# Adding an attention mask by accumulating DMAs instead of by a TensorE product per head

## The reference

```
x = relu(x + dt * stencil(x))                                   # layer 0
y = up(expert(gelu(down(x)))) + x                               # layer 1, the adapter
x = (y - mean(y)) * rsqrt(var(y) + eps) * ln_gamma + ln_beta    # per row: the adapter norm
x = x + two matmuls, each before a silu of a whole-sequence norm  # layer 2
x = ln(x) * (1 + scale) + shift; q, k, v of 16 heads of 16      # layer 3
scores = q k^T / 4 + attention_bias                             # bias: 16 x 16 x 256 x 256, fp32
scores = where(mask, -inf, scores)                              # mask: one 256 x 256 per sequence
x = x + softmax(scores) v Wo;  x + ff(ln(x))
```

## Time and profile before

| | |
|---|---|
| median of three runs | 944.76 us (942.92 to 946.6) |
| the profiled execution | 941.49 us, of it span 939.7 us |
| mean granted clock of TensorE | 0.975 of full speed (1.00 from 150 us on) |
| DMA | 130.88 MB in 133081 packets, mean 139 GB/s |
| first head starts | about 92 us |

### The profile page before, as it was taken

The page is one execution under the profiler, slowest core; times in us unless marked ns, Lnnn a source line. Parts: engine busy times, 40 slices in busy tenths (PEclk is TensorE's granted clock), DMA queues, the critical chain, the costliest instruction groups (busy, mean ns, idle before and its releaser), DMA issues.

```text
span 939.7 us, 18088 instructions
## 1 busy us (share of the span) xinstructions
PE 858.8 (91%) x5646; PEld 661.4 (70%) x5731; DVE 751.3 (80%) x2375; ACT 731.6 (78%) x1901; POOL 239.2 (25%) x237
## 2 busy tenths in 40 slices
PE   7675869999999999999999999999999999998987
PEld 6353646777777777777777777777777777776766
DVE  7466788988898889888898888888898889876542
ACT  3123879979798888979798888979798888987773
POOL 1233213222223224222223224222223224120100
PEclk9678899999999999999999999999999999999999
DMA  9814545645446353644446363644447353645500
GB/s 252 246 54 114 173 125 146 177 138 152 114 122 193 102 162 103 191 133 139 127 124 191 103 160 103 193 139 139 121 127 189 106 159 103 179 136 150 154 13 22
DMA packets 133081, 130.88 MB, mean 139 GB/s; under 512 B 18265, under 2 KB 123481, under 8 KB 132969
## 3 DMA queue, kind: packets, MB, share of 16 engines
q1 hardware_dynamic: 101072, 111.49, 42.1%
q10 hardware_dynamic: 31914, 18.23, 6.8%
HBM read 112.61 MB, written 17.07 MB: 138 GB/s over the span
## 4 chain that ended last, share of the span: by engine, by line
PE 48%; ACT 23%; DVE 18%; issue 8%; POOL 1%; DMA 1%; ACTq 0%; DVEq 0%; POOLq 0%
PE ff_ps L1335 11%; PE PT_ps L1371 6%; ACT Pr L1057 5%; PE ff_ps L1316 5%; DVE bias L921 4%; PE ctx_ps L1393 4%; PE G L1216 4%; PE scores_ps L1356 4%; PE G L1139 3%; ACT L1057 3%; ACT tanh L1039 3%; ACT PT L1070 3%; ACT ffT L1043 3%; PE scores_ps L1353 2%; PE G L1212 2%
## 5 line engine op out<-in xcount | busy, mean ns | idle before, releaser
L1057 ACT ACTIVATE Pr<-bias,nmax 128x256 f32<-128x256 f32 x512 | 255.9, 506 | 41.9 <-DVE nmax L921 41.4
L921 DVE CUSTOM_DVE_ANT_0 bias<-scores_ps,bias 128x256 f32<-128x256 f32 x512 | 195.4, 420 | 60.0 <-issue 35.4
L1070 ACT ACTIVATE PT<-PT_ps 128x512 f32<-128x512 f32 x256 | 151.7, 593 | 50.3 <-PE PT_ps L1371 41.0
L1371 PE MATMUL PT_ps<-ident,Pr 128*128 128x128 f32 x1024 | 156.4, 275 | 9.0 <-ACT Pr L1057 9.0
L559 POOL TENSOR_TENSOR rstd<-var,half_neg 128x2 f32<-128x2 f32 (+1 forms) x64 | 42.7, 667 | 403.5 <-DVE var L684 256.4
L1371 PEld LDWEIGHTS PT_ps<-ident,Pr 128*128 128x128 f32 x1024 | 119.8, 141 | 18.4 <-ACT Pr L1057 15.0
L1316 PE MATMUL ff_ps<-ctxT,w 128*128 128x256 f32 x480 | 116.9, 386 | 10.7 <-ACT ffT L1043 8.9
L1335 PE MATMUL ff_ps<-w,ffT 128*128 128x256 f32 x480 | 114.8, 382 | 0.3 <-DVE ffT L898 0.3
L1316 PEld LDWEIGHTS ff_ps<-ctxT,w 128*128 128x128 f32 x480 | 86.3, 190 | 30.2 <-ACT ffT L1043 14.2
L1356 PE MATMUL scores_ps<-k_stack,q_stack 96*128 96x256 bf16 x512 | 99.2, 275 | 6.7 <-issue 3.3
L1057 ACT ACTIVATION_READ_ACCUMULATOR Pr<-bias,nmax 128x1 f32 x512 | 100.8, 197 | 0.0
(11 more groups left out here) (219 smaller groups left out, 1628.6 us busy)
## 6 DMA issues: line engine op xcount, KB each, us to landing
bias<-in_fside_Bx16xSxS_dram SPq DMA_DIRECT2D x256, 256.0 KB, 3.2
part_dram<-front ACTq DMA_DIRECT2D x32, 384.0 KB, 3.5
q_stack<-part_dram SPq DMA_DIRECT2D x32, 192.0 KB, 3.3
k_stack<-part_dram SPq DMA_DIRECT2D x32, 192.0 KB, 3.9
F<-in_x_dram SPq DMA_DIRECT2D x16, 256.0 KB, 3.7
ada<-rows_dram SPq DMA_DIRECT2D x16, 256.0 KB, 4.5
q_stack<-part_dram SPq DMA_DIRECT2D x32, 128.0 KB, 3.6
k_stack<-part_dram SPq DMA_DIRECT2D x32, 128.0 KB, 3.8
```

The lines of the kernel that those rows point to most:

```text
L921: nc.vector.tensor_tensor_reduce(out=t, in0=SP_[:, n % 2, q * S:(q + 1) * S], in1=t, scale=-1.0, scalar=BIG, op0=ALU.add, op1=ALU.min, acc ...
L1057: ins = nc.scalar.activation(Pr[:, n % PR, q, :], bias[:, n // CH % RING, 2 * (n % CH) + q, :], ACT.Exp, bias=nmax[:, n, q:q + 1], scale=-1.0,
L1070: nc.scalar.activation(PT[:, m % BATCH, :, :].rearrange("p c q -> p (c q)"), TP[:, m % 2, :], ACT.Identity).then_inc(pt_ok, 1)
L1371: ins = pe.transpose(TP[:, m % 2, c * S + q * P:c * S + (q + 1) * P], Pr[:, m % PR, q, c * P:(c + 1) * P], ident[:, :])
```

## The change

The mask leaves TensorE. After the bias chunk has landed, GpSimd issues one DMA that reads the two mask tiles of the sequence (bf16) once for each of the chunk's two heads and adds them to the 512 KB of fp32 bias in SBUF. There is one such DMA per chunk, 128 in all, and it stands `ADD_AHEAD` = 4 heads ahead of its chunk's first head, at half a slot (`HEAD_AT`). VectorE waits for it instead of for the load. SP's list is unchanged. The next mask's tile is made once the last adds of the old one have landed.

The product of zeros is gone: the first large product opens the accumulation. The adapter norm is four passes over 128x256: subtract mean and multiply by gamma, for both tiles; then, after the reciprocal deviation, multiply by it and add beta. The tables have new numbers; two lines of them stand below.

```diff
-HEAD_AT = {"scores": 0, "turn_p": 0, "times_v": 0.25, ..., "masks": 0}
+HEAD_AT = {"scores": 0, "turn_p": 0, "times_v": 0.5, ..., "masks": 0, "add_mask": 0.5}
+ADD_AHEAD = 4
-      "xs": (9.5, 23.25), "inv0": (12, 30), "x2": (10.75, 24.75), "stat0": (11, 25), "avg0": (11.25, 27.25),
+      "xs": (9.75, 23.5), "inv0": (8.25, 22.75), "x2": (10.5, 24.25), "stat0": (11, 25.25), "avg0": (11.75, 27.75),
...
+        def chunks(j, c):
+            return j * (NCH // RING) + c // RING + 1
...
                 pool.wait_ge(mask_loaded, (j + 1) * 16)
                 if later(j):
-                    pool.wait_ge(score_mm, (j - 1) * HEADS + (b + 1) * H)
+                    for n in range(RING):
+                        pool.wait_ge(mask_added[n], chunks(j - 1, (b + 1) * NCH // 2 - RING + n) * 16)
...
+            def add_mask_to(j, c):
+                b, n = divmod(c, NCH // 2)
+                if n == 0:
+                    pool.wait_ge(mask_ok, 2 * j + b + 1)
+                pool.wait_ge(bias_loaded[c % RING], chunks(j, c) * 16 * CH)
+                pool.nop(nofuse=True)
+                both = window(mask_add[:, :, :], 2 * b * S, [[0, CH], [S, 2], [1, S]])
+                pool.dma_start(bias[:, c % RING, :, :].rearrange("p (n q) k -> p n q k", n=CH), both,
+                               accum_op=ALU.add).then_inc(mask_added[c % RING], 16)
...
+                if once("s_add", j, n):
+                    for c in range(ADD_AHEAD // CH):
+                        add_mask_to(0, c)
...
+            def add_mask(j, n, with_back):
+                h = n + ADD_AHEAD
+                if n < HEADS and h % CH == 0 and h // HEADS + j < PAIRS:
+                    add_mask_to(j + h // HEADS, h % HEADS // CH)
...
-                    dve.wait_ge(rstd_ok[b], 4 * j + 1)
...
-                    link(row_norm(xs[b], xs[b], mv[:, mine, :], rstd[:, b, :]))
-                    link(nc.vector.tensor_tensor(x2[b], xs[b], bc(ln_g[:, :], 2), ALU.mult))
-                    nc.vector.tensor_tensor(x2[b], x2[b], bc(ln_b[:, :], 2), ALU.add).then_inc(x2_ok, 1)
+                    for t in range(2):
+                        ins = nc.vector.scalar_tensor_tensor(out=x2[b][:, t, :], in0=xs[b][:, t, :], scalar=mv[:, 2 * b + t, 0:1],
+                                                             in1=ln_g[:, :], op0=ALU.subtract, op1=ALU.mult)
+                    link(ins)
+                    dve.wait_ge(rstd_ok[b], 4 * j + 1)
+                    for t in range(2):
+                        ins = nc.vector.scalar_tensor_tensor(out=x2[b][:, t, :], in0=x2[b][:, t, :], scalar=rstd[:, b, t:t + 1],
+                                                             in1=ln_b[:, :], op0=ALU.mult, op1=ALU.add)
+                    ins.then_inc(x2_ok, 1)
...
-                dve.wait_ge(bias_loaded[c % RING], (j * (NCH // RING) + c // RING + 1) * 16 * CH)
+                dve.wait_ge(mask_added[c % RING], chunks(j, c) * 16)
...
-                    pe.matmul(GF[b], zeros[:, :], bc(zeros[:, :], 2 * S // P), start=True, stop=False)
+                    for m, mat, x in ((0, gradT, X1), (0, lapT, p_b0), (1, gradT, X1)):
+                        pe.matmul(GF[b][:, m, :], mat[:, m, m * P:(m + 1) * P], x[b][:, m, :],
+                                  start=(m == 0 and mat is gradT), stop=False)
...
-                pe.matmul(SP_[:, h % 2, :], identb[:, :], mask_add[:, 2 * b:2 * b + 2, :].rearrange("p q k -> p (q k)"),
-                          start=True, stop=False)
                 for q in range(2):
                     ins = pe.matmul(SP_[:, h % 2, q * S:(q + 1) * S],
                                     stacks[0][:, b, hh, q * P:(q + 1) * P],
-                                    stacks[1][:, b, hh, :], start=False, stop=(q == 1))
+                                    stacks[1][:, b, hh, :], start=True, stop=True)
```

More of the change, by code:

```diff
@@ L70 @@
 TICKS = 4
-HEAD_AT = {"scores": 0, "turn_p": 0, "times_v": 0.25, "finish_ctx": 0, "bias_and_max": 0, "copy_pt": 0, "exps": 0,
-           "masks": 0}
-AT = {"x4": (28.75, 45.25), "ctx_spread": (18, 36.25), "ctx": (19.75, 36.5), "ctx_scale": (19.25, 36.25),
[4 rows of a table removed]
-      "w2": ((31, 32.5, 33, 35.25), (46.75, 47.25, 48, 51.5)), "out": (35.25, 51), "store": (39.25, 60.75),
-      "prods_p": (1.5, 14.5), "prods": (0.75, 13.75), "diffs": (2.75, 16), "edges": (2.75, 16.25), "l0": (4.75, 18.5),
-      "x1": (5.75, 18), "relu": (5.25, 18.75), "x1_turn": (7, 20.25), "x1T": (6.75, 20.25), "res1": (8.5, 24.75),
-      "down": (8.25, 21.5), "hid": (8, 20.5), "expert": (9.25, 22), "expT": (8.5, 21.5), "up": (9.25, 23.25),
[6 rows of a table removed]
-      "k_split": (26, 41.5), "k_out": (26, 41.25), "v": (28.75, 45.75), "V": (30.75, 45), "mask": (20, 2)}
@@ L103 @@
-AT_LAST = {"ctx_spread": (20.25, 52.75), "ctx": (20.25, 37), "ctx_scale": (20.25, 42), "wo": (21.5, 41.25),
[4 rows of a table removed]
-           "w2": ((31, 34.25, 47.25, 47.5), (59, 61.25, 68.25, 77)), "out": (54.75, 76), "store": (57.25, 63)}
+HEAD_AT = {"scores": 0, "turn_p": 0, "times_v": 0.5, "finish_ctx": 0, "bias_and_max": 0, "copy_pt": 0, "exps": 0,
+           "masks": 0, "add_mask": 0.5}
+ADD_AHEAD = 4
+AT = {"x4": (29.5, 39), "ctx_spread": (19.5, 36.75), "ctx": (20, 36.75), "ctx_scale": (20.25, 36.25), "wo": (21, 37),
[4 rows of a table added]
+      "w2": ((31, 33.25, 34.25, 35.5), (47, 47.75, 48, 51)), "out": (35.5, 51.75), "store": (45, 53.75),
+      "prods_p": (0, 13.5), "prods": (0.5, 12.75), "diffs": (2.5, 14), "edges": (3.75, 15.25), "l0": (4.75, 17.75),
+      "x1": (5.75, 18.75), "relu": (5, 18), "x1_turn": (7.25, 20.25), "x1T": (7, 20.25), "res1": (5.25, 20.25),
+      "down": (8.75, 21.5), "hid": (8.25, 20.75), "expert": (10, 22), "expT": (8.5, 21.75), "up": (10.25, 23.75),
[6 rows of a table added]
+      "k_split": (26.75, 41.5), "k_out": (26.75, 41.5), "v": (28.25, 43.25), "V": (29.5, 45.75), "mask": (20, 2)}
@@ L152, in adapter_to_attention_kernel @@
         gA0, gB0, gB1, gB2, gU, gW = (sb(n, [P, 2, D]) for n in ("gA0", "gB0", "gB1", "gB2h", "gU", "gW"))
-        zeros = sb("zeros", [1, P], BF16)
         edge1 = sb("edge1", [P, 2, 8])
@@ L313, in adapter_to_attention_kernel @@
         stack_loaded = [sem(f"stack_loaded{n}") for n in range(4)]
-        mask_ok, identb_ok = sem("mask_ok"), sem("identb_ok")
+        mask_ok = sem("mask_ok")
+        mask_added = [sem(f"mask_added{n}") for n in range(RING)]
         score_mm, biased, prob_ok, pt_tr, pt_ok, pv_mm, ctx_ok = (
@@ L637, in _ @@
                                     base=0, pattern=[[-1, P]], channel_multiplier=1).then_inc(const_set, 1)
-            nc.gpsimd.memset(zeros[:, :], 0.0).then_inc(const_set, 1)
             nc.gpsimd.memset(mean_mat[:, :], 1.0 / P).then_inc(const_set, 1)
@@ L642, in _ @@
             nc.gpsimd.memset(zero_eps[:, 1:2], EPS).then_inc(const_set, 1)
-            pool.wait_ge(const_set, 6)
-            run(pool, {"masks": masks}, front, back)
+            pool.wait_ge(const_set, 5)
+            run(pool, {"masks": masks, "add_mask": add_mask}, front, back)
         @block.vector
@@ L1213, in front @@
                                       x[b][far, 1 - m, :], start=False, stop=False)
-                    for m in range(2):
-                        for mat, x in ((gradT, X1), (lapT, p_b0)):
-                            ins = pe.matmul(GF[b][:, m, :], mat[:, m, m * P:(m + 1) * P], x[b][:, m, :],
-                                            start=False, stop=(m == 1 and mat is lapT))
-                    ins.then_inc(l0_mm, 1)
+                    pe.matmul(GF[b][:, 1, :], lapT[:, 1, P:2 * P], p_b0[b][:, 1, :],
+                              start=False, stop=True).then_inc(l0_mm, 1)
                 for b in seqs("x1_turn", j, n):
```

28 lines of the change are left out of this document (13 added, 15 removed), and 42 rows, old and new, of tables (AT, AT_FIRST, AT_LAST).

## The result

| | median, us | ratio to before (95% interval) |
|---|---|---|
| before, same chip | 943.84 (941.48 to 946.6) | |
| changed | 1007.62 (1000.08 to 1010.26) | 1.066 (1.0632 to 1.0687) |

The change costs 64 us; forecast were -26. The span of the profiled execution is 998.3 us, where 939.7 stood, and TensorE's mean granted clock 0.94 instead of 0.975. The first head starts at 88.9 us (92.0 before) and the last at 965.7 (907.1): all of the loss lies among the heads.

The account below looks back on a forecast made before the run. TensorE was taken to set the pace, with engines chained head by head. Mask and zeros products -30, norm -1, late adds +5, order 0 gave -26 us: 919 for the median, own range 899 to 938, whole range 884 to 985.

Parts of the forecast that it names:

- I take -30: TensorE's mask and zeros products removed: of 59.8 us, about half reaches the end, -30 us, ends 0 and -60.
- Rival (b): Nothing of TensorE's relief arrives, or the add's mechanism gives it back: 942 to 947 us, chance 0.15.
- 0 with -17 and +17: Slots of the hand-written tables move a little with the same dependences: 0 us, ends -17 and +17.
- I price this at nothing in the sum: GpSimd's add issues holding up VectorE's two-input passes, up to 1.1 us each: 0 in the sum, +25 at the upper end.
- The adds: GpSimd's accumulating DMAs: issue 1.2 us, landing 5.8, 7.0 together.
- Late adds (+5): At chunk 6, 7.0 us against 6.4 of room: 0.6 us wait per pair, +5 us, ends 0 and +26.
- Rival (c): DMA engines become the bound, destination read and written in two passes: 999 us; chance 0.23, shared with the adds' upper ends.
- The norm: VectorE's adapter norm: four passes, 1.64 us instead of 2.20 per sequence; -8 us of VectorE, -1 at the end.
- What the next profile was to show: If right: pair period near 102 us, DMA share 0.65 to 0.75; if wrong through the lock: long two-input VectorE passes beside adds.

Follow-up runs that it names:

- b_normzero: The kernel before with only the four-pass adapter norm and without the product of zeros; 939.07 us, ratio 0.9921.
- x_pemask: The changed kernel without accumulating DMAs, the mask added again by a TensorE product per head; 950.35 us, ratio 1.0059.
- x_noadd: The changed kernel with the accumulating DMAs left out, VectorE waiting for the bias load again, the mask in no score; 943.29 us, ratio 0.9992.
- x_tiny: The changed kernel with its 128 accumulating DMAs at the same places, but of 8 elements each instead of 512; 985.12 us, ratio 1.0424.
- x_busy: The changed kernel with each add replaced by two powers of 128x2 on GpSimd, the waits kept; 952.78 us, ratio 1.0082.
- x_waits: The changed kernel with all waits of the adds kept, but GpSimd only raising the semaphore in place of the DMA; 945.26 us, ratio 0.9981.
- y_gap_tiny: The changed kernel with adds of 8 elements, GpSimd waiting after each for its landing before its next product; 1107.44 us, ratio 1.1722.
- y_order: The changed kernel with four table numbers changed, putting GpSimd sums and layer-0 products ahead of layer 2's first deviation; 1032.6 us, ratio 1.0902.
- x_traffic: The changed kernel without adds, with one plain SyncE DMA per chunk from SBUF to DRAM ahead of its loads; 952.37 us, ratio 1.0064.

## Why the prediction was wrong

The measured terms, each from a difference of ratios: zeros and norm -7 (b_normzero), the new order +13 (x_pemask less b_normzero), the product -6 (x_noadd less x_pemask), sum 0; the issues +41 (x_tiny less x_noadd); the bytes +22 (after less x_tiny). Together +63, with rounding. The sum has to come out, since each term begins where the one before it ends; only the single terms are measurements.

- **"I take -30" for TensorE's product.** The first step that failed. It was worth 6 in the new order and 9 in the old. TensorE's 96% of the pair was no bound, and its 48% of the chain no exchange rate. I had read the evidence against it (the waits in the loop, rows 7) and taken a middle value. Rival (b)'s "nothing arrives" was the nearer.
- **"0 with -17 and +17" for the order.** Within its ends, near the upper.
- **"I price this at nothing in the sum" for VectorE's two-input passes.** The failed step that turned the sign: the adds' issues cost 41 us where the sum had nothing, and for that it gave no reason. The mechanism was named and given at most 1.1 us each, +25. Rows 14 showed one sum beside one pass; a run with an issue in it holds a pass for up to 5.3 us, and the place invites it: the pass that waits for the deviation starts just as the run behind that deviation does. Shown: a DMA is needed for it (x_busy, x_waits), and a follower without a gap (y_gap_tiny). In x_tiny line 712 grew by as much as all of VectorE's busy time did. Not shown is how much of it reached the end, since no run mends that pass without moving the harm, as y_order did. Why an issue joins what follows it into one long hold is not shown either.
- **The adds.** Issue 1.2, landing 5.8 against 1.24 and 6.1: right. Late adds (+5) were the only term for the bytes, and mis-sized: nine waits, 19 us of VectorE standing in all, and 22 us for the bytes in time. The 1.8 us of issue in this term's upper end stands in no row.
- **Rival (c).** Its 999 is near the result by chance: loads landed after 3.9 and not over 5 us, the share was 0.83, and a share of 0.93 costs 7. The bytes' +22 are then some 7 of plain traffic; the rest fits the late adds and longer loads of q and k (4.7 to 6.2 us, 3.4 to 4.2 in x_tiny), but was not taken apart.
- **The norm.** Four passes at 0.48 us, not 0.41: 1.92 for 2.20. With the zeros it gave 7, not 3.
- **What the next profile was to show.** The DMA share, "two-input VectorE passes long beside adds" and the clock were the telling rows; the clock (0.975 to 0.94) I had not named. What the clock costs was not tried by itself, so it stays a possible part of the issues' 41 us (0.944 in x_tiny, 0.956 in x_noadd).

The page "SBUF — State Buffer" of the Trainium skill, section "Who interferes with whom", says that a VectorE instruction with two SBUF inputs contends with a GpSimd instruction that reads SBUF, and that the second to come is blocked until the first finishes. x_noadd agrees: a pass that began 0.10 us after a sum of 1.28 us took 1.73 us. The kernel after does not: 5.30 us, through one issue and three sums. The same section says that a DMA does not contend with a compute engine; x_traffic agrees, with 763.0 us of VectorE against 762.2 in x_noadd.

## What to carry to other kernels

Before you credit a busy engine's relief, ask of the waits whether that engine sets the pace; here 50 to 60 us off any of three engines gave 4 to 9. Do not put DMA issues of GpSimd next to its sums or behind a result that VectorE is waiting for: what is queued behind such a result runs exactly beside its consumer. A lightly loaded engine can still be on the path through its latency; gaps and spacers there made it slower, and of three moves two did too and one changed nothing clear of noise.
